# Turning the probabilities of full key chunks by DMA transposes instead of TensorE transposes, in an attention and mixture-of-experts layer on one core

## What is computed

```python
xn = layernorm(x)                        # x: (2, 2048, 256) float32
scores = (xn @ W_qk) @ xn.T / 16 + (kpos - qpos) * slope   # causal mask
s = softmax(scores) @ (xn @ W_v.T)
probs = softmax(xn @ Wr); e = argmax(probs)    # top-1 of 8 experts
y = relu(xn[e's tokens, at most 512] @ W1[e]) @ W2[e] * prob
out = x + s * silu(y)
```

## Time and profile before

| what | value |
|---|---|
| median of 3 runs | 448.99 us (448.63 to 449.17) |
| the profiled execution's own time | 449.1 us |
| its span, first to last instruction | 447.4 us (1.7 us lie around it) |
| TensorE busy | 432.1 us, 97% of the span |
| VectorE, ScalarE, GpSimd busy | 326.9, 222.0, 227.9 us |
| granted TensorE clock, mean | 0.999 |
| DMA, whole program | 67.10 MB, mean 150 GB/s |

### The profile page before, as it was taken

The page is one execution under the profiler, slowest core; times in us unless marked ns, Lnnn a source line. Parts: engine busy times, 40 slices in busy tenths (PEclk is TensorE's granted clock), DMA queues, the critical chain, the costliest instruction groups (busy, mean ns, idle before and its releaser), DMA issues.

```text
span 447.4 us, 8558 instructions
## 1 busy us (share of the span) xinstructions
PE 432.1 (97%) x3142; PEld 301.2 (67%) x3142; DVE 326.9 (73%) x839; ACT 222.0 (50%) x436; POOL 227.9 (51%) x360
## 2 busy tenths in 40 slices
PE   5799899999999999999999999999999999999997
PEld 2377576777678766776776666666666666676776
DVE  5989777877898578767756977879796967425553
ACT  1755364353655346544444545555455545456441
POOL 5247860834735736054100667665757475748510
PEclk9999999999999999999999999999999999999999
DMA  7992845023722533252717495766768863232101
GB/s 239 356 356 75 239 122 185 1 79 65 269 75 49 109 130 97 67 204 73 122 7 247 107 315 177 246 232 188 267 160 282 169 201 106 96 111 78 52 13 35
DMA packets 68249, 67.10 MB, mean 150 GB/s; under 512 B 37231, under 2 KB 62076, under 8 KB 66160
## 3 DMA queue, kind: packets, MB, share of 16 engines
q1 hardware_dynamic: 56944, 44.19, 34.0%
q0 software_dynamic: 5824, 16.74, 11.9%
q10 hardware_dynamic: 5440, 5.64, 3.9%
HBM read 31.33 MB, written 28.58 MB: 134 GB/s over the span
## 4 chain that ended last, share of the span: by engine, by line
PE 83%; DVE 7%; DMA 5%; ACT 2%; issue 1%; another core or an unknown queue 1%; SPq 0%; DVEq 0%
PE bank L1283 20%; PE bank L1285 19%; PE bank L1284 19%; PE bank L1353 6%; PE bank L1368 6%; PE bank L1371 6%; PE bank L1370 6%; DMA sc<-in_w_e 3%; DVE sc L921 1%; DVE pT_l L937 1%; DMA xg<-in_x 1%; DMA sc<-in_w_r 1%; DMA tops<-wmax 1%; ACT sc L1166 1%
## 5 line engine op out<-in xcount | busy, mean ns | idle before, releaser
L1172 ACT ACTIVATE pT_h<-bank 128x512 f16<-128x512 f32 (+2 forms) x80 | 42.4, 532 | 81.6 <-PE bank L1353 77.8
L1368 PE MATMUL bank<-v_h,pT_h 128*128 128x257 f16 x272 | 74.6, 274 | 0.3 <-DVE pT_l L937 0.2
L1371 PE MATMUL bank<-v_h,pT_l 128*128 128x257 f16 x272 | 74.1, 272 | 0.0
L1370 PE MATMUL bank<-v_l,pT_h 128*128 128x256 f16 x272 | 73.7, 271 | 0.0
L1184 ACT ACTIVATE hid_h<-bank 128x512 f16<-128x512 f32 x64 | 38.0, 595 | 65.8 <-PE bank L1285 62.5
L1283 PE MATMUL bank<-w_h,hid_h 128*128 128x256 f16 x256 | 69.8, 273 | 0.0
L1285 PE MATMUL bank<-w_h,hid_l 128*128 128x256 f16 x256 | 69.8, 273 | 0.0
L1284 PE MATMUL bank<-w_l,hid_h 128*128 128x256 f16 x256 | 69.8, 273 | 0.0
L937 DVE SCALAR_TENSOR_TENSOR pT_l<-bank,pT_h 128x512 f16<-128x512 f32 (+2 forms) x80 | 48.6, 607 | 28.9 <-ACT pT_h L1172 26.9
L1007 DVE SCALAR_TENSOR_TENSOR hid_l<-bank,hid_h 128x512 f16<-128x512 f32 x64 | 43.8, 684 | 35.0 <-ACT hid_h L1184 29.0
L921 DVE CUSTOM_DVE_ANT_0 sc<-bank,bias,score_mul 128x512 f32<-128x512 f32 (+2 forms) x80 | 52.9, 664 | 7.1 <-PE bank L1285 6.7
(11 more groups left out here) (181 smaller groups left out, 909.0 us busy)
## 6 DMA issues: line engine op xcount, KB each, us to landing
raw<-in_w_e SPq DMA_DIRECT2D x5, 2048.0 KB
sc<-in_w_e SPq DMA_DIRECT2D x3, 2048.0 KB
slots<-empty ACTq DMA_DIRECT2D x1, 4224.0 KB, 19.4
gates<-gate SPq DMA_DIRECT2D x8, 512.0 KB
out<-xg SPq DMA_DIRECT2D x7, 512.0 KB
rows<-xg SPq DMA_DIRECT2D x7, 512.0 KB
rows<-so SPq DMA_DIRECT2D x7, 512.0 KB, 3.0
xg<-in_x SPq DMA_DIRECT2D x6, 512.0 KB, 4.2
```

Of the source, the lines that this page charges most:

```text
L1172: a_.activation(pT_h[:, t % 2, c * GTOK:c * GTOK + w], tr_ps[n % 2][:, 0:w], ACT.Copy, scale=P_UP).then_inc(pT_hi, 1)
L1368: pe.matmul(pv_ps[t % 2][:, 0:D + 1], pT_h[:, t % 2, rows_], v_h[:, at, q, 0:D + 1], start=kb == 0, stop=False)
L1370: pe.matmul(pv_ps[t % 2][:, 0:D], pT_h[:, t % 2, rows_], v_l[:, at, q, :], start=False, stop=False)
L1371: last = pe.matmul(pv_ps[t % 2][:, 0:D + 1], pT_l[:, t % 2, rows_], v_h[:, at, q, 0:D + 1], start=False, stop=kb == t % NT)
```

## The change

In tiles with three or four chunks (tile 27 excepted) all chunks but the last, 38 in all, are no longer turned by TensorE. ScalarE and VectorE split the probabilities where they stand in `sc`, in rows, and write both halves into one of two buffers `p_rows`; SyncE then turns both halves with one DMA transpose of 128x1024 float16 into `pT`, whose layout now holds the two halves of a block side by side. `values` waits for that transfer (`pT_in`) instead of for `low`. The DMA transposes of x of group 5 move from tile 13 to tile 14.

```diff
-        pT_h = sb("pT_h", [P, 2, S], F16)
-        pT_l = sb("pT_l", [P, 2, S], F16)
+        pT = sb("pT", [P, 2, NT, 2, P], F16)
...
+        p_rows = [sb(f"p_rows{k}", [P, GT, 2, P], F16) for k in range(2)]
...
+        def by_dma(t, c):
+            if t == REST - 1:
+                return False
+            return c in {3: (0, 1), 4: (0, 1, 2)}.get(chunks(t), ())
...
+            def chunk_turn(t, c):
+                i = dma_no(t, c)
+                sp.wait_ge(pT_lo, chunk_no(t, c) + 1)
+                sp.wait_ge(pv_full, t - 1)
+                sp.dma_start_transpose(pT[:, t % 2, c * GT:c * GT + GT, :, :].rearrange("p b h t -> p (b h) t"),
+                                       p_rows[i % 2][:, :, :, :].rearrange("p b h t -> p (b h t)")
+                                       ).then_inc(pT_in[i % 2], 16)
...
+                for c in steps(t):
+                    if by_dma(t, c):
+                        chunk_turn(t, c)
                 for n in (*SPLIT_TILE, LATE):
-                    if t == SPLIT_TILE.get(n, REST - 8):
+                    if t == {5: 14, LATE: REST - 8}.get(n, SPLIT_TILE.get(n)):
                         turn(n)
...
+            for t in range(REST, TILES):
+                for c in steps(t):
+                    if by_dma(t, c):
+                        chunk_turn(t, c)
...
             def high(t, c):
-                act.wait_ge(turned, n + 1)
-                a_.activation(pT_h[:, t % 2, c * GTOK:c * GTOK + w], tr_ps[n % 2][:, 0:w], ACT.Copy, scale=P_UP
+                if by_dma(t, c):
+                    i = dma_no(t, c)
+                    act.wait_ge(exp_made, n + 1)
+                    if i >= 2:
+                        act.wait_ge(pT_in[i % 2], i // 2 * 16)
+                    hi, _ = row_halves(t, c)
+                    p = sc[:, t % 2, chunk_cols(t, c)]
...
             def values(t, c):
-                pe.wait_ge(pT_lo, n + 1)
+                if by_dma(t, c):
+                    i = dma_no(t, c)
+                    pe.wait_ge(pT_in[i % 2], i // 2 * 16 + 16)
+                else:
+                    pe.wait_ge(pT_lo, n + 1)
...
-                    if c < chunks(t):
+                    if c < chunks(t) and not by_dma(t, c):
                         turn(t, c)
```

More of the change, by code:

```diff
@@ L296, in layer_kernel @@
         pT_lo = sem("pT_lo")
+        pT_in = [sem(f"pT_in{k}") for k in range(2)]
         pv_full = sem("pv_full")
@@ L349, in last_step, with turn_no, dma_no, chunk_cols @@
             return c == len(steps(t)) - 1
+        def by_dma(t, c):
+            if t == REST - 1:
+                return False
+            return c in {3: (0, 1), 4: (0, 1, 2)}.get(chunks(t), ())
+        def turn_no(t, c):
+            return sum(not by_dma(k, m) for k in range(t) for m in range(chunks(k))) + sum(not by_dma(t, m) for m in range(c))
+        def dma_no(t, c):
+            return chunk_no(t, c) - turn_no(t, c)
+        def chunk_cols(t, c):
+            return slice(c * GTOK, c * GTOK + chunk_blocks(t, c) * P)
+        def turned_halves(t, c):
+            at = pT[:, t % 2, c * GT:c * GT + chunk_blocks(t, c), :, :]
+            return at[:, :, 0, :], at[:, :, 1, :]
+        def row_halves(t, c):
+            k = dma_no(t, c) % 2
+            return p_rows[k][:, :, 0, :], p_rows[k][:, :, 1, :]
+        def in_blocks(ap):
+            return ap.rearrange("p (b t) -> p b t", t=P)
         def units_after(t, c):
@@ L526, in _ @@
             spread(1)
-            sp.wait_ge(turned, chunk_no(REST, 0))
+            sp.wait_ge(turned, turn_no(REST, 0))
+            sp.wait_ge(pT_lo, chunk_no(REST, 0))
             sp.dma_start(sc[:, :, :], w_k[2]).then_inc(w_in[0], 16)
@@ L1170, in high @@
                 n, w = chunk_no(t, c), chunk_blocks(t, c) * P
-                act.wait_ge(turned, n + 1)
-                a_.activation(pT_h[:, t % 2, c * GTOK:c * GTOK + w], tr_ps[n % 2][:, 0:w], ACT.Copy, scale=P_UP
-                              ).then_inc(pT_hi, 1)
+                if by_dma(t, c):
[4 more added lines that the diff above has]
+                    hi, _ = row_halves(t, c)
+                    p = sc[:, t % 2, chunk_cols(t, c)]
+                else:
+                    act.wait_ge(turned, turn_no(t, c) + 1)
+                    hi, _ = turned_halves(t, c)
+                    p = tr_ps[n % 2][:, 0:w]
+                a_.activation(hi, in_blocks(p), ACT.Copy, scale=P_UP).then_inc(pT_hi, 1)
             def split_high(buf, e, k, q):
@@ L1366, in values @@
                     kb = c * GT + q
[L1367 to L1368 removed]
+                    p_h, p_l = pT[:, t % 2, kb, 0, :], pT[:, t % 2, kb, 1, :]
+                    pe.matmul(pv_ps[t % 2][:, 0:D + 1], p_h, v_h[:, at, q, 0:D + 1],
                               start=kb == 0, stop=False)
[L1370 to L1371 removed]
+                    pe.matmul(pv_ps[t % 2][:, 0:D], p_h, v_l[:, at, q, :], start=False, stop=False)
+                    last = pe.matmul(pv_ps[t % 2][:, 0:D + 1], p_l, v_h[:, at, q, 0:D + 1],
                                      start=False, stop=kb == t % NT)
```

7 lines of the change are left out of this document (4 added, 3 removed).

## The result

The changed kernel took 463.35 us (median of 4 runs, 461.31 to 463.74) beside 448.81 for the one before on the same chip: a ratio of 1.0315, with a 95% interval from 1.0298 to 1.0332. It is slower, as forecast, but by 14.5 us and not by 5.3, and above the range. The profiled execution took 463.74 us (span 462.0).

What follows compares the result with a forecast made beforehand. TensorE, busy 97% of the span, was taken as the bound. Tiles 8 to 10 −2.6, 11 to 16 +8.9, 24 to 26 −2.0, 28 to 31 +1.0 gave +5.3 us: 454.3 us, range 446 to 462 (8 in 10).

Steps and rivals of the forecast that it cites:

- What is removed: 38 chunks of four transposes at 0.433 us each, 16.5 us of TensorE in tiles 8 to 15, 24 to 26, 28 to 31.
- step (a): Tile 12: first chunk lands late, behind the transposes of group 4's x on SyncE; TensorE stalls 2.3 us.
- the prediction's count: Times in us from the start of tile 11, written with "+".
- issue in proportion: Rival: a chunk's issue grows to 2.56 us, landing 4.0, every wait at its upper bound; 464 us, chance 0.22.
- Steps (b) to (d): Tiles 13, 14 and 16: late chunk transfers and in-order waits stall TensorE 3.2, 5.1 and 4.3 us.
- (d): Tile 16: tile 15's three chunks come out behind the transposes of group 5's x; stall 4.3 us.
- the walk: Step-by-step carrying of issues, landings and in-order waits through the tiles; its stalls minus the transposes removed give +5.3 us.
- VectorE's wait for x in tile 13: Sign for the forecast: group 4's load, issued at +26.7, makes VectorE stand until +30.9 in tile 13.
- the sum: Total over all tiles: −2.6 + 8.9 − 2.0 + 1.0 = +5.3 us.
- Step (e): Tiles 24 to 26: SyncE has little else there, so 2.0 of the 2.6 us removed are gained.
- Step (f): Tiles 28 to 31: two buffers and landings cost 6.2 us of stalls against 5.2 removed; +1.0 us.
- the in-order waits do not reach TensorE: Rival: ScalarE gets its buffer back early and VectorE's reads stay ahead; 442.5 us, chance 0.24 for all that is faster.

Runs made afterwards that it cites:

- tail_only: Changed kernel with only the 12 chunks of tiles 28 to 31 by DMA, those of tiles 8 to 26 on TensorE as before: 453.84 us.
- tail_by_pe: Changed kernel with all chunks of tiles 28 to 31 turned on TensorE again, the 26 of tiles 8 to 26 still by DMA: 454.24 us.
- all_gates_late: Changed kernel with all 38 transfers, VectorE scaling the gathered last gates behind tile 30 rather than 29: 459.34 us.
- late_filled: all_gates_late plus unread matrix products, seven and nine, in two TensorE gaps of the last tile: 457.28 us.
- only_8_10_24_26: Changed kernel with only the twelve chunks of tiles 8 to 10 and 24 to 26 by DMA, the others on TensorE: 442.49 us.

## Why the prediction was wrong in size

- **What is removed, tiles 8 to 10, and step (a):** right. Tile 11 started 2.64 us sooner (2.6 said), tile 13 began at +22.4 on the prediction's count (22.0 said). The landing of an undisturbed chunk was 3.3 us (issue 99.25, first values at 102.53; 3.2 said), but by another sum: the issue is 1.23 us and not 1.9, so it did not grow from 128x512 (1.28) to 128x1024, and the rest is 2.0 and not 1.3. The rival "issue in proportion" is out by this row, though its time (464) is near what was measured. The data moved at 181 to 208 GB/s at a full DMA share (three windows from 100.5 to 103.2). The Trainium skill (Advanced Engine Details and Errata, X-Bar Transpose) expects 350 to 400 GB/s; the trace does not agree.
- **Steps (b) to (d):** the mechanism was right, and the runs with two chunks and with four buffers show it (6 to 9 us of 11.5). The size, from tile 11 to tile 17, was +12.7 in place of +8.9. Tile 12's first chunk landed 9.4 us behind the broadcast's issue (105.29 to about 114.7) where I had 7.9, so tile 14 began at +37.6 for 36.0. group_in(5) was issued 8.4 us behind group_out(5) (118.67 to 127.05) where I had 6.2, so tile 13's first chunk came 3 us later than in the walk, and `rmin` of tile 14 came 6.2 us into the tile, not 5.2. VectorE's wait for x in tile 13, a sign that I had named, was there with 0.56 us only (to 121.89). For (d) TensorE waited 0.8 and 1.0 us for tile 15's chunks where I had 4.3, and 1.3 for VectorE. That the clock falls behind such gaps was not in the sum at all: 1.7 us at 154 to 158.
- **Step (e):** −3.3 between tiles 17 and 28 where I said −2.0; without the 1.0 us that tail_only gains there too, it is −2.3. Three more executions with the same chunks (tail_by_pe, all_gates_late, late_filled) gave −4.5 in place of −3.3. In only_8_10_24_26 tiles 24 to 26 gave −3.8, of which 0.4 is again what tail_only gains; why the rest is more than the 2.6 of their transposes was not pursued.
- **Step (f), the failed step:** "the end 1.0 to 1.3 us later: +1.0". It was +7.9, 6.9 of the 9.3 us by which the trace missed the sum. The walk itself held: with the gates late, the last four tiles alone took 41.30 us in the trace, 1.2 more than before, `rmin` of tile 31 came 1.7 us sooner (1.0 said), and from it to the last product it was 14.9 us (14.4 said). What the step had left out, and so put at nothing, is first VectorE's wait for the gathered gates at line 1160. Before, it stood 1.40 us there with time to spare. Now the first part of the gather was issued 14.0 us behind the start of tile 28's step in place of 13.1 (424.50, and 416.82 before), and its last part was there 4.8 us behind its issue in place of 2.7, with chunk data moving beside it. That, with the clock behind it, is 47.93 − 43.47 = 4.5 us of the trace, and 3.4 to 4.2 us of the time. Second, 43.47 − 41.08 = 2.4 us in the last tile, 1.7 of it the lower clock and 0.8 the later third chunk. That is also what makes the end dearer in the whole kernel than alone, where the clock stood at 1.00 in the last tile; why it fell in one and not in the other, behind gaps of 2.0 and 2.6 us and of 2.0 and 1.8, no run separates.
- **The rivals:** "the in-order waits do not reach TensorE" is true of twelve of the 38 chunks (tiles 8 to 10 and 24 to 26), where SyncE's queue has room.

Left open: why the gather lands later with the chunks (shared DMA engines, or the queue's own order), since only the chunks' presence was varied. And whether any order of SyncE's queue saves tiles 12 to 15.

## What to carry to other kernels

A DMA that relieves the bounding engine has to be priced by everything that waits in order behind it: the engine that refills its source buffer, that engine's next reader, and the queue that issues it. Walk the whole program for in-order waits that are met today with a microsecond or two to spare, since a shift anywhere can put them on the path; here one of them cost about 4 us, and moving one line removed it. Where gaps open on TensorE, add the clock to their price, and apply the change only to the tiles in which the queue is idle.

## What I had not expected of the hardware

- A transpose of 128x1024 from SBUF takes 1.23 us to issue, as one of 128x512 did (1.28), and its values start 3.3 us behind its issue when undisturbed, 8.0 behind a megabyte of plain stores in the same queue.
- TensorE's granted clock fell behind gaps of 1.3 to 4.5 us, but not behind each (behind 2.8 us at tile 13 in one run, not behind 3.6 us in another). By the estimate from the windows it cost 1.7 us in most places and 3.4 behind the longest gap, of 4.5 us. Seven and nine products into an idle bank kept it up in the last tile.
- GpSimd's operations of 128x256 (lines 768 and 770), of 0.73 us otherwise, took 1.18 and 1.20 us once each at the start of the last tiles (413.06 and 414.32), beside VectorE's new remainders that read and write SBUF. That these are the cause is not shown: tail_only has 1.19 us once at 367.74, where no chunk goes by DMA.
